# Cross attention with a routed feed-forward layer: another order of TensorE's steps, the K bank used alone, and loads in another order

## What is computed

```python
def _L0_xattn_ref(query, key, value, Wq, bq, Wk, bk, Wv, bv, Wo, bo):
    Q = query @ Wq.T + bq
    K = key @ Wk.T + bk
    V = value @ Wv.T + bv
    ...  # split in 16 heads of 16
    energy = jnp.einsum('bhqd,bhkd->bhqk', Q, K) / scale
    attn = jax.nn.softmax(energy, axis=-1)
    x = jnp.einsum('bhqk,bhkd->bhqd', attn, V)
    x = x.transpose(0, 2, 1, 3).reshape(B, S, HIDDEN)
    return x @ Wo.T + bo

x = x + _L0_xattn_ref(_layernorm(x), ctx_1024, ctx_1024, ...)
# for each token: scores = x @ wr + br, the best expert's gelu(x @ w1 + b1) @ w2 + b2
x = x + _L0_ffn_ref(_layernorm(x), ...)
```

## Time and profile before

| what | value |
|---|---|
| median of 3 runs | 394.64 us (394.29 to 395.02) |
| the profiled execution | 395.08 us |
| its span, first to last instruction | 393.4 us |
| mean granted TensorE clock | 0.953 |
| TensorE busy (multiplications) | 331.1 us, 84% |
| VectorE / GpSimd / ScalarE busy | 155.8 / 152.2 / 139.2 us |

### The profile page before, as it was taken

One profiled execution on the slowest core, in us unless ns is written; L12 is line 12 of the kernel. 1 busy time (PEld: TensorE's weight loads), 2 busy tenths in 40 slices (PEclk: granted clock), 3 DMA queues, 4 the chain that ended last, 5 costly groups with the idle time before them and its releaser, 6 DMA issues. The chain is left out here.

```text
span 393.4 us, 9142 instructions
## 1 busy us (share of the span) xinstructions
PE 331.1 (84%) x3283; PEld 282.4 (72%) x3283; DVE 155.8 (40%) x349; ACT 139.2 (35%) x426; POOL 152.2 (39%) x382
## 2 busy tenths in 40 slices
PE   0378999999999999987341999999999999999992
PEld 0356677777777777755211989999999999999991
DVE  1134766666666777676291111121111111211210
ACT  0245555555545555543000522332422423323320
POOL 4433666666665666442257772211111112112111
PEclk9999999999999999999555899999999999999998
DMA  6970044434440000001009899445354454463300
GB/s 187 319 260 2 17 143 130 131 131 129 132 137 30 28 29 28 28 36 48 27 7 343 252 356 317 137 149 190 128 185 161 135 194 142 139 219 133 116 0 0
DMA packets 28698, 51.87 MB, mean 132 GB/s; under 512 B 3117, under 2 KB 18607, under 8 KB 28528
## 3 DMA queue, kind: packets, MB, share of 16 engines
q1 hardware_dynamic: 24720, 43.00, 33.1%
q0 software_dynamic: 2944, 8.13, 6.2%
q10 hardware_dynamic: 992, 0.17, 0.3%
HBM read 45.01 MB, written 7.21 MB: 133 GB/s over the span
## 5 line engine op out<-in xcount | busy, mean ns | idle before, releaser
L428 ACT ACTIVATE hT<-bank,b_sb 128x128 f32<-128x128 f32 x184 | 52.6, 369 | 106.2 <-PE bank L832 106.2
L832 PEld LDWEIGHTS bank<-xeT,w_slot 128*128 128x128 f32 x736 | 87.5, 196 | 2.4 <-DMA w_slot<-in_w 1.3
L832 PE MATMUL bank<-xeT,w_slot 128*128 128x128 f32 x736 | 87.7, 279 | 0.9 <-DMA w_slot<-in_w 0.9
L846 PE MATMUL bank<-w_sb,hT 128*128 x368 | 83.1, 379 | 0.0
L846 PEld LDWEIGHTS bank<-w_sb,hT 128*128 128x128 f32 x368 | 68.2, 190 | 8.4
L316 POOL DMA_INDIRECT out<-y_sb,scatter_i x23 | 22.7, 987 | 128.8 <-DVE y_sb L622 122.3
L479 DVE TENSOR_REDUCE peaks<-bank 128x4 f32<-128x512 f32 x64 | 39.8, 684 | 8.1 <-PE bank L648 8.1
L607 DVE COPY xeT<-bank 128x256 f32<-128x256 f32 x23 | 9.8, 425 | 83.1 <-PE bank L822 83.1
L385 ACT ACTIVATE probsT<-bank 128x512 f32<-128x512 f32 x64 | 33.0, 602 | 13.7 <-PE bank L724 13.7
L622 DVE TENSOR_TENSOR y_sb<-gathered,bank 128x256 f32<-128x256 f32 x23 | 9.7, 421 | 57.2 <-PE bank L846 57.2
L364 ACT ACTIVATE k_pair<-bank,bk_pair,own 128x128 f32<-128x128 f32 x64 | 24.1, 457 | 21.0 <-PE bank L689 21.0
(11 more groups left out here) (124 smaller groups left out, 426.8 us busy)
## 6 DMA issues: line engine op xcount, KB each, us to landing
w_slot<-in_w SPq DMA_DIRECT2D x23, 1024.0 KB, 4.9
w_sb<-in_w SPq DMA_DIRECT2D x8, 1024.0 KB, 5.7
records<-record SPq DMA_DIRECT2D x16, 256.0 KB, 2.0
gathered<-in_x SPq DMA_DIRECT2D x3, 512.0 KB, 7.8
gathered<-in_ctxT SPq DMA_DIRECT2D x3, 512.0 KB, 7.4
b_sb<-in_b SPq DMA_DIRECT2D x1, 1024.0 KB, 9.3
gathered<-records,gather_i POOLq DMA_INDIRECT x23, 6.1
out<-y_sb,scatter_i POOLq DMA_INDIRECT x23, 2.4
```

Source lines behind the costliest of these rows:

```text
L428: ins = a.activation(hT[:, s % 2, c], H_BANK[s % 2][c // 4][:, P * (c % 4):P * (c % 4 + 1)], ACT.Gelu, bias=b1_sb[:, bass.ds(e * FC + c, 1)])
L832: ins = t.matmul(H_BANK[s % 2][f // 4][:, P * (f % 4):P * (f % 4 + 1)], w1_slot[:, s % 2, c, P * f:P * (f + 1)], xeT[:, s % 2, c], start=( ...
L846: ins = t.matmul(Y_BANK[s % 2][:, 0:D], hT[:, s % 2, c], w2_flat[:, bass.ds(e * (FC * D) + c * D, D)], start=(c == 0), stop=(c == FC - 1))
```

## The change

The loads on SyncE's queue are issued in another order (x of a group apart from its context). GpSimd makes the identity and one mask index first, then normalises two batches, and makes its other constants between. The bias bv gets a semaphore of its own, so the masks and ScalarE wait for five small loads instead of six. ScalarE runs one exponential on a single column after it has issued its loads. The transposed input moves from `K_BANK` to the second half of `M_BANK`, and the product with Wo from `K_BANK` to `U_BANK`; so `K_BANK` is left to K, and `weigh_values` waits for the residual of the batch before instead of for its division. K and Q are projected two batches ahead of the scores, where K was one and Q two ahead; x is transposed three ahead (was two). The first batches are written out ahead of the loops, which now start at 0. No instruction of the computation is added or taken away but for that one exponential.

```diff
--- before
+++ after
@@ sync
-            load_inputs(0)
+            load_x(0)
+            load_weight(wk_sb, wkT, "wk_in")
+            load_ctx(0)
             load_weight(wq_sb, wqT, "wq_in")
-            load_weight(wk_sb, wkT, "wk_in")
+            load_x(1)
             load_weight(wv_sb, wvT, "wv_in")
-            load_inputs(1)
+            load_ctx(1)
+            load_x(2)
             load_weight(wo_sb, woT, "wo_in")
-            load_inputs(2)
+            load_ctx(2)
...
@@ gpsimd
-            pool.wait_ge(sm["masks_done"], 6)
-            for b in range(-3, LAST):
+            pool.wait_ge(sm["consts_pool"], 2)
+            normalize_x(0)
+            normalize_x(1)
+            attention_constants()
+            pool.wait_ge(sm["masks_done"], 5)
+            own_queries(0)
+            routing_constants()
+            normalize_x(2)
+            for b in range(LAST):
+                if live(b + 3):
+                    normalize_x(b + 3)
                 if live(b - 2):
                     normalize_x1(b - 2)
                 if live(b + 1):
                     own_queries(b + 1)
-                if live(b + 3):
-                    normalize_x(b + 3)
                 if live(b):
                     add_bo(b)
@@ scalar
-            act.dma_start(bv_col[:], ...).then_inc(sm["bias_in"], 16)
+            act.dma_start(bv_col[:], ...).then_inc(sm["bv_in"], 16)
...
-                a.copy(xnT[:], K_BANK[:, 0:D].rearrange("p (c s) -> p c s", c=KC)).then_inc(sm["xT_taken"], 1)
+                a.copy(xnT[:], M_BANK[:, D:2 * D].rearrange("p (c s) -> p c s", c=KC)).then_inc(sm["xT_taken"], 1)
...
             def take_x2T(b):
                 act.wait_ge(sm["x2T_ready"], b + 1)
+                wait_for(act, "xT_ready", b + 6)
...
+            act.wait_ge(sm["consts_pool"], 1)
+            a.activation(warm[:], minus_half[:], ACT.Exp)
+            act.wait_ge(sm["bias_in"], 16 * 5)
...
@@ vector
-                v.tensor_tensor(record[:, b % RECORDS, 0:D], K_BANK[:, 0:D], x_all[:, b], ALU.add).then_inc(sm["x1_done"], 1)
+                v.tensor_tensor(record[:, b % RECORDS, 0:D], U_BANK[:, 0:D], x_all[:, b], ALU.add).then_inc(sm["x1_done"], 1)
...
-            for b in range(-2, LAST):
+            stats_x(1)
+            spread_bv()
+            stats_x(2)
+            stats_x(3)
+            dve.wait_ge(sm["consts_pool"], 3)
+            for b in range(LAST):
...
-                if live(b + 3):
-                    stats_x(b + 3)
+                if live(b + 4):
+                    stats_x(b + 4)
@@ tensor, waits
             def weigh_values(b):
...
-                wait_for(pe, "o_done", b)
+                wait_for(pe, "x1_done", b)
...
             def project_k(b):
...
-                wait_for(pe, "xT_taken", b + 1)
-                wait_for(pe, "x1_done", b - 2)
+                wait_for(pe, "k_taken", b)
...
             def turn_x(b):
                 pe.wait_ge(sm["xn_done"], b + 1)
-                wait_for(pe, "k_taken", b)
+                wait_for(pe, "q2_done", b - 2)
...
             def project_o(b):
                 pe.wait_ge(sm["o_done"], b + 1)
-                wait_for(pe, "xT_taken", b + 4)
-                wait_for(pe, "k_taken", b + 3)
-                wait_for(pe, "x1_done", b)
                 for c in range(KC):
-                    ins = t.matmul(K_BANK[:, 0:D], oT[:, c], ...)
+                    ins = t.matmul(U_BANK[:, 0:D], oT[:, c], ...)
```

More of the change, by code:

```diff
@@ L238, in _ @@
-            g.affine_select(out=before[:], in_=before[:], compare_op=ALU.is_ge, fill=0.0, base=-1,
-                            pattern=[[1, P]], channel_multiplier=-1)
-            g.memset(ones[:], 1.0)
-            g.memset(minus_half[:], -0.5)
-            for i in range(PAIR):
-                g.memset(ones_pair[:, i, HD * (PAIR - 1 - i):HD * (PAIR - i)], 1.0)
-            g.iota(iota_i[:], pattern=[[1, P]], base=0, channel_multiplier=0)
-            g.iota(iota_part_i[:], pattern=[[1, 1]], base=0, channel_multiplier=1)
@@ L254, in _, with attention_constants @@
-            g.tensor_copy(slot_f[:], slot_i[:]).then_inc(sm["consts_pool"], 1)
+                            pattern=[[-1, P]], channel_multiplier=1).then_inc(sm["consts_pool"], 1)
+            def attention_constants():
+                g.memset(peaks[:], 0.0)
+                g.memset(v_pair[:], 0.0)
+                g.memset(ones_pair[:], 0.0)
+                g.memset(before[:], 1.0)
+                g.memset(ones[:], 1.0)
+                g.memset(ends[:], 0.0).then_inc(sm["consts_pool"], 1)
@@ new lines, in routing_constants @@
+            def routing_constants():
+                pool.wait_ge(sm["consts_pool"], 3)
+                for i in range(PAIR):
+                    g.memset(ones_pair[:, i, HD * (PAIR - 1 - i):HD * (PAIR - i)], 1.0)
+                g.affine_select(out=before[:], in_=before[:], compare_op=ALU.is_ge, fill=0.0, base=-1,
+                                pattern=[[1, P]], channel_multiplier=-1)
+                g.iota(iota_i[:], pattern=[[1, P]], base=0, channel_multiplier=0)
+                g.iota(rev_i[:], pattern=[[-1, E]], base=E, channel_multiplier=0)
+                g.iota(tok_i[:], pattern=[[P, NB]], base=1, channel_multiplier=1)
+                g.iota(slot_i[:], pattern=[[1, SLOTS_W]], base=0, channel_multiplier=0).then_inc(sm["consts_pool"], 1)
+                pool.wait_ge(sm["consts_pool"], 4)
+                g.tensor_copy(iota_row[:], iota_i[:])
+                g.tensor_copy(iota_part[:], iota_part_i[:])
+                g.tensor_copy(rev[:], rev_i[:])
+                g.tensor_copy(tok1[:], tok_i[:])
+                g.tensor_copy(slot_f[:], slot_i[:]).then_inc(sm["consts_pool"], 1)
@@ L399, in take_q @@
                 ins.then_inc(sm["q_taken"], 1)
-            act.wait_ge(sm["bias_in"], 16 * 6)
+            act.wait_ge(sm["consts_pool"], 1)
+            a.activation(warm[:], minus_half[:], ACT.Exp)
+            act.wait_ge(sm["bias_in"], 16 * 5)
             act.wait_ge(sm["masks_done"], 6)
-            for b in range(-3, LAST):
+            take_k(0)
+            take_xT(0)
+            take_q(0)
+            take_xT(1)
+            act.wait_ge(sm["consts_pool"], 3)
+            take_v(0)
+            take_k(1)
+            take_q(1)
+            take_xT(2)
+            for b in range(LAST):
                 if live(b - 3):
@@ L521, in _ @@
                     stats_x1(b - 1)
+            dve.wait_ge(sm["consts_pool"], 5)
             n = [0]
@@ L710, in turn_x @@
                 pe.wait_ge(sm["xn_done"], b + 1)
-                wait_for(pe, "k_taken", b)
+                wait_for(pe, "q2_done", b - 2)
                 wait_for(pe, "xT_taken", b)
+                wait_for(pe, "x2T_taken", b - 5)
                 for c in range(KC):
-                    ins = t.transpose(K_BANK[:, P * c:P * (c + 1)], xn[:, b % 2, P * c:P * (c + 1)], ident[:])
+                    ins = t.transpose(M_BANK[:, D + P * c:D + P * (c + 1)], xn[:, b % 2, P * c:P * (c + 1)], ident[:])
                 ins.then_inc(sm["xT_ready"], 1)
@@ L749, in project_o @@
                 pe.wait_ge(sm["o_done"], b + 1)
[L750 to L752 removed]
                 for c in range(KC):
[L754 removed]
+                    ins = t.matmul(U_BANK[:, 0:D], oT[:, c], wo_sb[:, c], start=(c == 0), stop=(c == KC - 1))
                 ins.then_inc(sm["y_ready"], 1)
@@ L762, in project_bv @@
                 ins.then_inc(sm["bv_ready"], 1)
-            pe.wait_ge(sm["consts_pool"], 3)
-            for b in range(-2, LAST):
+            pe.wait_ge(sm["consts_pool"], 2)
+            project_k(0)
+            turn_x(0)
+            project_q(0)
+            turn_x(1)
+            for b in range(LAST):
                 if live(b):
                     scores(b)
+                if b == 0:
+                    project_v(0)
+                    project_k(1)
+                    project_q(1)
+                    turn_x(2)
+                    project_bv()
                 if live(b - 1):
```

73 lines of the change are left out of this document (35 added, 38 removed).

## The result

The changed kernel takes **381.74 us** (median of 4 runs, 380.69 to 382.44) against 394.47 us (394.14 to 395.02) of the kernel before beside it: ratio 0.9674, 95% interval 0.9644 to 0.9703. A second series of six runs gave 383.66 us (380.84 to 384.87) against 394.86: ratio 0.9701 (0.9666 to 0.9737).

A forecast was written before the change was run, and what follows sets the result against it. The attention was taken as bound by a chain through K's evacuation, plus a late start. Gains of 6.5 (start) and 3.95 (loop) less 0.4 (last weighing) made 10.0 us, giving 384.7 us, range 382.2 to 388.2.

The forecast's parts named there:

- The chain through K's bank: Attention loop: x's transposition waits for K's evacuation, exponentials end just before the next scores; one closed chain of 9.98 us.
- The period's size: Attention loop: with K off the chain, one batch takes 9.74 us instead of 9.98; gain 3.95 us.
- VectorE's chain: Attention loop: product with Wo, residual, maxima and back through TensorE's steps, 9.70 us, as long as TensorE's sum.
- The last period: Last of the 14 periods from second to last scores: 8.60 us, as K, Q and x are gone.
- The start: Up to the second scores: 27.0 instead of 33.54 us, gain 6.5, limited by GpSimd's constants and normalisation of batch 2.
- The table load: ScalarE's start: one early exponential takes the activation table load of 1.28 us off the path.
- The last weighing: End of the attention: it now waits for the residual, which costs 0.4 us.
- I take zero: Rest of the tail, routing and feed-forward: no change, though the clock may shift them by a us either way.
- 0.8 us: Whole kernel: about 0.2% is what a measurement can tell from no change.
- a low clock at the start: Rival, chance 0.13: low pace lasts to batch 1, the start gains 3.4 instead of 6.5, total 387.8 us.
- no gain in the period: Rival, chance 0.12: another wait of about 0.3 replaces the removed one, period 9.98, gain 0.8, total 387.9 us.
- both better: Rival, chance 0.09: period 9.6 and an early high clock at the start, total 382.2 us.

The follow-up runs named there:

- x3_k_ahead: Changed kernel with K of batch b+2 back between routing and the transposed maxima, in its own bank: 378.53 us (ratio 0.9602).
- x12_filled: Changed kernel with 9 additional identity products ahead of K(0) and 16 between x(0)'s transposition and Q(0): 383.92 us (ratio 0.9705).
- x4_k_split: Changed kernel with K(b+2) in two halves, four products ahead of the transposed maxima and four behind V: 376.64 us (ratio 0.9561).
- x15_k_split2: Changed kernel with K in two halves and nothing else, run a second time: 378.65 us (ratio 0.9564).
- x7_warm: Changed kernel with ten products of the identity with itself on TensorE ahead of K(0): 384.89 us (ratio 0.9746).
- x14_both: Changed kernel with split K, only K and Q biases awaited, batch 2 normalised straight after batch 1, 11 and 10 additional products: 377.63 us (ratio 0.9531).
- x8_all: Changed kernel with K in two halves, 9 and 7 additional products at the start, only K and Q biases awaited there: 378.86 us (ratio 0.9591).
- x13_start: Changed kernel with 11 and 14 additional products at the start and GpSimd normalising batch 2 straight after batch 1: 381.87 us (ratio 0.9633).

## Why the prediction was right or wrong

- **The chain through K's bank** was right: period 9.98 before; no wait at x's transposition after; exponentials off the chain.
- **The period's size** was wrong, and this is the step that failed: 9.74 forecast, 9.55 measured, which is 2.3 of the 2.8 us by which the gain of the profile pair exceeds the forecast one. The mis-sized terms of the sum are the two transpositions, "0.27" and "0.33", which measured 0.21 and 0.22. The other terms came within 0.01, and the product with Wo, which I had between 0.88 and 1.03 without a row that shows it free of waits, took 0.96. In the kernel before, the 0.33 stood behind a wait and ahead of the 32-row products of the shifted scores; the 0.27 stood behind no wait, but straight behind those products. What a wait adds the transposed maxima show: 0.27 behind one (97.67 to 97.94), 0.22 without (95.05 to 95.27 in `x3_k_ahead`). What the 32-row neighbours add to a transposition no run separates, so the cause of these 0.17 is shown in part only. The rest is the 0.04 that I had put on top of the sum of 9.70. The lower bound of 9.6 was not low enough for the same reason.
- **VectorE's chain**, also given as 9.70, had the same two terms in it. It was real but not binding: 0.1 of slack.
- **The last period** (8.60 forecast) measured 159.59 - 150.99 = 8.60.
- **The start**: scores(0) 14.6 forecast, 14.23; scores(1) 27.0, 27.32. That the times fit is in part luck. K(0) came at 6.20, not 7.75 (7.19 in the second profile): it started 4.5 us after the context's issue, for which I had taken the 6.0 of a weight twice its size. The wait for GpSimd that I had named as the limit did not show, since TensorE's low pace, through ScalarE's queue, made up the same time; `x12_filled` shows that wait, at 20.27.
- **The table load** took 1.28 and the exponential behind it started 0.01 later. As in the kernel before, no drain of the kind that the Trainium skill, ScalarE: Activation LUTs, section What ACT_TABLE_LOAD costs, puts beside it is to be seen.
- **The last weighing**: cost 0.4 forecast, 0.50 measured (9.01 less 8.51).
- **"I take zero"** for what lies behind: 1.0 of gain in the profile pair, of which 0.84 is between the first gather and the first product. Over the 16 profiles that stretch took 7.4 to 9.1 us, 8.2 in the second one of the changed kernel, so it is spread and no effect of the change to be told. The clock's fall at the end of the attention, which I had put at a us either way, is worth up to 2.7 us between two executions of one program (20.73 and 23.42, `x4_k_split` and `x15_k_split2`). So "0.8 us" for what a measurement can tell was too little: the two series of the changed kernel lie 1.9 us apart.
- **The rivals**: a low clock at the start was there up to 19.7 and priced in; none in the loop; "no gain in the period" did not come; "both better" (382.2) came nearest in number, but the early clock that it rested on did not come.

What stays open: why the clock falls at 165 us in one execution and at 174 in another of the same program, whether the new order makes the early fall likelier, what a transposition costs beside 32-row products, and whether the last weighing's bank is worth its 0.5 us.

## What to carry to other kernels

Before a step is moved past an engine's wait, ask whether it is held there by its place or by a buffer that it shares: here K left where it was, in a bank of its own and with the transposition of x moved, gave more than the change. Once a queue runs without waits, the prices to add up are those of steps that follow each other without a wait, with the neighbours that they will have. Read behind a wait or beside 32-row products, a short transposition looked a quarter to a half too long here (0.27 and 0.33 against 0.21 and 0.22). At a start, look for a second chain of the same length before one is shortened: an engine made faster only waits, here long enough for its clock to fall again.

## What the runs showed of the hardware

- TensorE's products took twice as long at the start, where the work came in pieces, though the granted clock was recorded as 1.00 there (the third value from the end, in the changed kernel). This lasted until 19.7 us in one execution of the changed kernel and 18.3 in the other, where K(1) already took 1.05:

```profile
12.00:18.00 6.00, 5.71 (x30) 4.24 (x29) 2.16 (x5) 0.89 (x3) 5.61 (x25) 1.00 1.15 316
```

  With additional products ahead, K(0) ran in 1.13 us at 6.1 us, and the long products came back behind idle times of 4.36 us (`x7_warm`), 2.70 (`x12_filled`), 2.53 (`x14_both`) and 2.33 (`x8_all`, there 1.2 us after the work had begun again), but not behind the 1.43 us of `x13_start`.
- Eight products of 128x128 take 0.99 from start to start behind the 32-row products of the shifted scores (K in the changed kernel, Q in `x4_k_split`), and 0.90 behind eight of their own kind (Q behind K). Behind the small products of `route`, K takes 0.97 (`x3_k_ahead`).
- The same program's clock fell to half at 165.0 us in one execution and at 173.6 in another, and the end of the attention was 2.5 us longer in the first.
